# Who writes the high fp16 halves of the expert weights: five of twelve experts move from ScalarE to GpSimd

## The reference

```
x = x + 0.5 * moe(layernorm(x))       # call 0 of the expert layer
x = x + attention(layernorm(x))
x = x + 0.5 * moe(layernorm(x))       # call 1, the same weights

moe: probs = softmax(h @ Wr + br); top 3 of 12 experts
     w_e   = mean over the tokens of expert e of softmax(top 3 values)
     out   = sum over e of mask_e * w_e * (relu(h @ w1[e] + b1[e]) @ w2[e] + b2[e])
     out  *= 1 - 0.8 * (phi(mean over tokens of out) > 0.7)
```

## Time and profile before

| | us |
|---|---|
| median of 3 runs | 795.31 |
| the profiled execution | 794.92 |
| its span | 793.1 |
| PE busy | 628.5 (79%) |
| DVE busy | 493.3 (62%) |
| POOL busy | 370.9 (47%) |
| ACT busy | 330.9 (42%) |

### The profile page before, as it was taken

One profiled execution on the slowest core, in us unless ns is written; L12 is line 12 of the kernel. 1 busy time (PEld: TensorE's weight loads), 2 busy tenths in 40 slices (PEclk: granted clock), 3 DMA queues, 4 the chain that ended last, 5 costly groups with the idle time before them and its releaser, 6 DMA issues.

```text
span 793.1 us, 21180 instructions
## 1 busy us (share of the span) xinstructions
PE 628.5 (79%) x7596; PEld 549.7 (69%) x7597; DVE 493.3 (62%) x1033; ACT 330.9 (42%) x934; POOL 370.9 (47%) x258
## 2 busy tenths in 40 slices
PE   1414677999999997559999997129999999999853
PEld 1313666998999997137888885028999999999711
DVE  6897896554454454068898988973544555455405
ACT  2977986444434443013232323026444444444300
POOL 0004166888888885101101000023888888888510
PEclk9756899999999999669999997558999999999967
DMA  9995723465665443810000003003444444444383
GB/s 300 374 371 173 219 43 52 95 126 112 132 125 114 92 74 41 232 53 2 2 0 0 0 2 107 1 27 121 67 75 73 77 70 71 74 71 72 48 231 106
DMA packets 72583, 79.79 MB, mean 101 GB/s; under 512 B 6304, under 2 KB 64928, under 8 KB 72160
## 3 DMA queue, kind: packets, MB, share of 16 engines
q0 software_dynamic: 22656, 30.95, 23.8%
q1 hardware_dynamic: 49888, 48.35, 18.7%
HBM read 48.08 MB, written 31.20 MB: 100 GB/s over the span
## 4 chain that ended last, share of the span: by engine, by line
PE 62%; DVE 16%; issue 7%; ACT 5%; DMA 5%; SPq 3%; ACTq 1%; DVEq 1%; POOL 0%; POOLq 0%
PE PS L810 59%; PE PS L867 3%; ACT A L715 2%; DMA expert_sums<-A,place 2%; DVE W L1222 2%; DVE A L1374 2%; DMA W<-w 1%; SPq L450 1%; DMA A<-expert_sums 1%; ACT A L597 1%; DVE A L1371 1%; DVE A L1575 1%; ACT W L605 1%; ACT A L641 1%; SPq L452 1%
## 5 line engine op out<-in xcount | busy, mean ns | idle before, releaser
L810 PE MATMUL PS<-A,W 128*128 128x128 f16 (+1 forms) x3796 | 247.6, 227 | 16.3 <-DVE W L1222 12.0
L810 PEld LDWEIGHTS PS<-A,W 128*128 (+1 forms) x3796 | 238.9, 107 | 22.7 <-DVE W L1222 12.9
L527 POOL DMA_INDIRECT A<-xn_rows,token x118 | 162.7, 1379 | 184.1 <-DVE token L1397 124.1
L810 PE MATMUL PS<-W,A 128*128 (+1 forms) x1898 | 236.9, 280 | 6.9 <-DVE A L1443 3.5
L545 POOL DMA_INDIRECT expert_sums<-A,place x118 | 194.9, 1652 | 73.8 <-issue 40.3
L715 ACT ACTIVATE A<-PS,b1s 128x128 f32<-128x128 f32 x590 | 159.2, 391 | 157.7 <-PE PS L810 157.7
L810 PEld LDWEIGHTS PS<-W,A 128*128 128x128 f16 (+1 forms) x1898 | 191.3, 104 | 33.9 <-issue 5.4
L1433 DVE CAST A<-A 128x1280 f16<-128x1280 f32 x58 | 50.0, 861 | 191.8 <-ACT A L715 191.8
L810 PE MATMUL PS<-A 32*128 32x128 f32 (+3 forms) x1248 | 65.9, 282 | 32.1 <-DVE A L1374 24.9
L1435 DVE TENSOR_TENSOR A<-A 128x1280 f16<-128x1280 f32 x58 | 86.6, 1493 | 2.0
L810 PEld LDWEIGHTS PS<-A 32*128 32x128 f32 (+3 forms) x1248 | 52.0, 150 | 43.8 <-DVE A L1374 29.8
(11 more groups left out here) (161 smaller groups left out, 423.9 us busy)
## 6 DMA issues: line engine op xcount, KB each, us to landing
W<-w SPq DMA_DIRECT2D x24, 640.0 KB, 11.1
A<-expert_sums SPq DMA_DIRECT2D x16, 512.0 KB, 7.3
expert_sums<-zeros SPq DMA_DIRECT2D x2, 2304.0 KB, 18.6
expert_sums<-zeros SPq DMA_DIRECT2D x12, 384.0 KB
xn_rows<-A SPq DMA_DIRECT2D x8, 512.0 KB, 6.9
A<-b SPq DMA_DIRECT2D x2, 1536.0 KB, 7.7
X<-x SPq DMA_DIRECT2D x4, 512.0 KB, 6.0
out<-X SPq DMA_DIRECT2D x8, 256.0 KB, 2.6
```

The costliest lines, as they stand in the source:

```text
L527: nc.gpsimd.indirect_dma_start(XG[q][:, u * D:(u + 1) * D], None, xn_dram[:, :], bass.IndirectOffsetOnAxis(ap=token[:, at:at + 1], axis=0) ...
L810: return nc.tensor.matmul(out_, l, r, start=start, stop=stop_, skip_group_check=True)
```

## The change

POOL gets the high parts of the experts 3, 5, 7, 9 and 11, ACT keeps those of 0, 1, 2, 4, 6, 8 and 10. POOL's instruction computes the same as ACT's, in the same size. It signals on a semaphore of its own, `w_hi_pool`, and DVE's `low_parts` waits for that one or for `w_hi` by the expert.

```diff
+        BY_POOL = tuple(range(3, E, 2))
...
+            def high_parts(e):
+
+                for n, (raw, half) in enumerate(((W1, w1h), (W2, w2h))):
+                    pool.wait_ge(w_lo, e * 4 + (2 * n + 1))
+                    pool.sem_inc(pool_held, 1)
+                    nc.gpsimd.tensor_scalar(half[:, e * 2 * SLOT:e * 2 * SLOT + SLOT],
+                                            raw[:, e * SLOT + SLOT:e * SLOT + 2 * SLOT], wscale[:, e, n:n + 1], None,
+                                            ALU.mult).then_inc(w_hi_pool, 1)
...
                 for b in range(LAG):
                     gather(f, b)
+                    if f == 0 and b == LAG - 1:
+                        high_parts(BY_POOL[0])
                 pool.wait_ge(sums_cleared[f], 16 * LANES * (1, CLEARS)[f])
                 for b in range(NB):
                     if b + LAG < NB:
                         gather(f, b + LAG)
+                    if f == 0 and b < RAMP:
+                        high_parts(BY_POOL[b + 1])
                     scatter(f, b)
...
                     high_parts(2)
                     for m in range(2):
                         square_sum(10, m)
-                    high_parts(3)
                     relu(0, 0)
...
                         high_parts(2 * b + 4)
-                        high_parts(2 * b + 5)
...
                 for n, (raw, cut) in enumerate(((W1, w1h), (W2, w2h))):
-                    dve.wait_ge(w_hi, e * 2 + (n + 1))
+                    if e in BY_POOL:
+                        dve.wait_ge(w_hi_pool, 2 * BY_POOL.index(e) + (n + 1))
+                    else:
+                        dve.wait_ge(w_hi, 2 * (e - sum(p < e for p in BY_POOL)) + (n + 1))
```

More of the change, by code:

```diff
@@ L310, in build @@
         w_hi = sem("w_hi")
+        w_hi_pool = sem("w_hi_pool")
         w_lo = sem("w_lo")
@@ L603, in high_parts @@
                 for n, (raw, half) in enumerate(((W1, w1h), (W2, w2h))):
+                    assert e not in BY_POOL
                     act.wait_ge(w_lo, e * 4 + (2 * n + 1))
```

## The result

The changed kernel takes 833.76 us, the median of 5 runs (832.41 to 837.79), where the kernel before took 796.09 (795.23 to 799.47, 5 runs). The ratio is 1.048, with a 95% interval of 1.045 to 1.051: 37.7 us slower. The forecast was 824, with a range of 814 to 838.

The account below looks back on a forecast made before the run. DVE was taken to bound the ramp. Expert 5's low parts end at 102.6 us; three iterations of 18.3 lead to 157.5 against 128.2, so 29.3 more than 794.92: 824 us, range 814 to 838.

Parts of the forecast that it names:

- The rival of no change: Behind the ramp the delay is caught up; PE's idle time gives at best 3.5 us of 29.3; chance 0.02.
- The clears ahead of expert 5: In POOL's list gather(4) waits for the cleared sums, so expert 5's high parts start at 96.2; low parts end 7.5 us later.
- The circle: In the ramp, scatter, gather, high parts, low parts, split and weigh wait in turn: 18.3 us an iteration, was 10.9; chance 0.52.
- Expert 3: At the ramp's start its high parts come earlier on POOL, moving the start a little forward, worth nothing in the end.
- Serial rather than side by side: In the ramp DVE's low parts and POOL's high parts exclude each other, so DVE waits 2T, 2.8 us, rather than T.
- The time T of a high part: One POOL instruction of 128 x 1280 takes 1.4 us, between a lower end of 1.16 and an upper end of 3.6.
- 146.3 + 4k: General sum for the ramp's end in us; k is the time from POOL's first high part to DVE's start on it.
- The fixed part of the circle: What a ramp iteration takes besides the two high parts: DMA instructions, gaps, low pieces, split and weigh, 15.5 us.
- Side by side: Rival: POOL and DVE do not disturb each other in the ramp, k = 1.4, ramp's end 151.9, 818.6 us; chance 0.30.
- The slow high part with exclusion: Rival: POOL's high part takes 3.6 us and excludes DVE, k = 7.2, 841.8 us; slow POOL's chance 0.11.
- Faster: Rival: odd experts' high parts are ready early, POOL is off the path, the cast's waits go: about 791 us; chance 0.02.
- ACT's relu: In the ramp DVE's cast waits for it 0.83, 0.82 and 1.61 us; moving work off ACT can give back 3.3 us.

Follow-up runs that it names:

- clears later: Changed kernel, but POOL waits for the cleared sums ahead of scatter(0) instead of ahead of gather(4): 833.69 us, ratio 1.047 to the kernel before.
- late scatters: Changed kernel with each POOL high part from expert 5 on one place earlier in POOL's list, ahead of the scatters: 819.60 us, ratio 1.029 to the kernel before.
- turns: Changed kernel, but POOL writes W2's high part only after DVE has written both low pieces of W1: 837.32 us, ratio 1.053 to the kernel before.
- memset: Changed kernel, but POOL's high part is a memset to zero instead of the multiply: 814.54 us, ratio 1.022 to the kernel before.
- copy: Changed kernel, but POOL's high part is a copy from fp32 to fp16 without the multiply: 821.58 us in a single run.
- tensor_tensor: Changed kernel, but POOL multiplies by a tensor_tensor with the scale broadcast over 1280 columns: 828.83 us, ratio 1.039 to the kernel before.
- bias first: Kernel before, nothing on POOL, but ACT weighs the biases ahead of the odd expert's high parts instead of behind them: 797.55 us, ratio 1.000.

## Why the prediction came out as it did

**The chain and the bound: right.** DVE bounds the ramp, the ramp's delay goes whole into the time, nothing is caught up. 38.4 us at the ramp's end, 37.7 between the medians. The rival of no change is out.

**The clears ahead of expert 5: right.** gather(4) at 93.20, its high parts at 95.50 (forecast 96.2). The run with the clears later puts their part of the loss at 2.6 us, since without them the meeting with the low parts of expert 4 holds expert 5 up: its two high parts take 8.31 us there, from 90.09 to 98.40.

**The circle: right.** Cast to cast grew from 10.9 to 20.6, and the late scatters, which cut the circle, bring it to 15.6 (what else that edit moves, the place of expert 5, lies ahead of these turns). The low end for any such circle was given wrongly in the prediction: DMA instructions, low pieces, split and weigh make 14.0 us, and only with the 0.9 ahead of the scatter 14.9. Nothing hangs on it, both are far from 10.1.

**Expert 3: wrong, but it cost little.** I said that its high parts would come earlier and move the start of the ramp forward. They did come earlier, but they met the low parts of expert 2, and the first cast came 3.1 us later (86.14 against 83.05). I had priced this meeting for expert 5 and forgot it here. The clears hid it; where only expert 3 is on POOL, 0.7 us of it are left at the ramp's end.

**Serial rather than side by side: right, and now shown.** DVE starts on W1 while POOL is in W2's part, and its first piece ends 0.2 us after POOL does: 99.07 + 3.70 = 102.77 against 95.50 + 7.03 = 102.53. A piece that began only when POOL's record ends would have ended 0.9 us after it, so the two are serial but for some tenths. No meeting, no long piece (turns); no reading, no long piece (memset); reading, a longer piece (copy, tensor_tensor).

**The time T of a high part: wrong, and the number that moved the forecast.** I took 1.4 us, near the memset, and it is 3.5, at my upper end. In the sum 146.3 + 4k, with k = 2T, that is 4 x (7.05 - 2.8) = 17.0 us. The reason I gave, one input instead of two, was wrong twice. The operation decides, not the count of inputs: copy 1.25, add 2.32, `tensor_scalar` 3.5. And the upper end was made wrongly. Five times the 725 ns of the add of 256 elements gave 3.6 us, near the truth of another operation; the add of 1280 takes 2.32, so by these two about 0.33 us of the 725 ns is fixed (an estimate, since the operands differ). The estimate of 1.1 us plus a start that stands beside T in the prediction fits the copy and the memset, not the multiply.

**The fixed part of the circle: too large, and it hid nearly half of that.** I had 15.5 + 2T. Measured it is 20.6 - 7.05 = 13.5. The four DMA instructions took 6.7 to 6.9 us and not 7.5 (109.04 to 115.76). There is no 0.3 us between the gather and the high part. And DVE's first piece has been issued by the time that POOL ends, so that only 105.16 - 102.53 = 2.6 us of low parts follow, not 3.6. With the true T my formula would give 146.3 + 4 x 7.05 = 174.5 for the ramp's end, 8 us too late; with my T it gave 157.5, 9 too early. That the time, 833.76, fell inside 814 to 838 is in part luck: one error of 17.0 us and one of 7.9 the other way. The order of events was forecast rightly and the loss too small, 29.3 us of 37.7. Of the signs that I named, the DVE waits of 6 to 8 us came (6.89 to 7.67); the turn (17 to 18.5), the end of expert 5's low parts (101 to 103, measured 105.2) and the ramp's end (152 to 158) did not.

**The rivals.** Side by side (0.30) is out by the long piece. The slow high part with exclusion, which had a chance of 0.11 with the other slow case, is what happened; its price of 842 was 8 us too high for the reason just given. Faster (0.02) would have needed a circle of 10.1 us; not even the memset comes near.

**ACT's relu.** I priced the relief of ACT at 3.3 us at most if nothing came for it. The run with the bias first takes the waits away, and nothing is left of it in the time. So the 791 us of the rival "faster" (794.9 - 3.3 is 791.6) would not have come either.

## What to carry to other kernels

An engine with idle time is not a place for work: look at what stands ahead of the new instruction in its list and at who waits for what comes behind, since two engines that wait for each other in turn add up all that lies between. Then add up the list of the engine that gets the work: here its DMA instructions and two multiplies make 14.0 us a turn, more than the 10.1 of the engine that was the limit. POOL and DVE are not independent either, so an instruction that POOL takes over from ACT can be paid for on DVE. An instruction that the trace does not have should be priced by its operation, and where only other operations are there, the upper bound deserves as much weight as the lower.

## What the runs showed of the hardware

- POOL, 128 x 1280 fp32: memset 1.16 to 1.18 us, copy 1.25, `tensor_tensor` 2.32 to 2.33, `tensor_scalar` 3.44 to 3.67 (4.0 to 4.7 where a DVE low piece was already running), whatever the output type and whether the scalar is a constant or from memory. ACT does the same multiply in 1.36.
- A DVE instruction with two inputs from SBUF is held while POOL reads: 3.70 us instead of 0.88 in the changed kernel. Beside POOL's memset it keeps 0.88. The Trainium skill, "SBUF — State Buffer", section "Who interferes with whom", has this rule, and the traces agree with both halves of it. That the lock lasts for the whole instruction, as the prediction quotes it, they do not quite bear out: beside instructions of 3.5, 2.3 and 1.2 us the piece got 2.82, 2.05 and 0.97 us longer.
- DVE's `tensor_scalar` from SBUF to SBUF in fp32, one input, is held as well: 17.21 us instead of 2.67 for eight of them beside POOL's multiplies and copies. So is one of 12 elements in int32, 3.30 us instead of 0.17.
- When DVE has a queue of pieces and POOL wants to read, they alternate: eight pieces and two multiplies took 12.0 us, where one after the other would be 6.45 + 7.05 = 13.5. POOL's two multiplies take 8.31 us there instead of 7.05.
